# Self-attention scores of a fused decoder layer, made for two key heads at a time instead of one

## The chip, the cores and the metric

The kernel runs on one core of a Trainium2 chip. The metric is the device time of one launch in microseconds (us); three launches of the kernel before were timed. The engines of the core run side by side and meet at semaphores: TensorE (PE, with its weight loads listed as PEld), VectorE (DVE), ScalarE (ACT), GpSimd (POOL) and SyncE (SP), which issues the DMAs.

## What is computed

A decoder layer for 8 sequences of 128 positions with 512 features, in float32: layer norm and causal self-attention, cross-attention over a context, and a feed-forward part. The change concerns only the scores of the self-attention, which has 32 query heads of 16 features and 8 key heads, four query heads to each key head. Cut to what matters:

```python
q = q * cos + _rotate_half(q) * sin
k = k * cos + _rotate_half(k) * sin
qg = q.reshape(b, HKV, G, t, DH)              # HKV = 8, G = 4, DH = 16
scores = einsum('bhgtd,bhkd->bhgtk', qg, k) / sqrt(DH)
scores = where(causal, scores, finfo(float32).min)
attn = softmax(scores, axis=-1)
ctx = einsum('bhgtk,bhkd->bhgtd', attn, v)
```

## The kernel before

**Arithmetic.** Every float32 product is made of three matmuls of a reduced-precision type: each operand is held as a high part (suffix h) and the remainder (suffix l), and `split3` (L217) issues high x high (L219), high x low (L220) and low x high (L221). ScalarE writes each high part (`hi`, L982), VectorE each low part (`lo`, L1218).

**Stages.** A self-attention stage runs over the 8 sequences (`batch`, one call to a sequence; seven go through a hardware loop, the last is written out). Behind it come a cross-attention stage and a feed-forward stage, which the change doesn't touch. A batch also makes the keys and values that its sequence needs in the cross-attention (`cross_values`, `cross_keys`), and the projections of the next sequence (`turn_xn`, `q_product`, `kv_product`, `turn_qk`).

**Scores.** `scores(b, j)` makes the scores of key head j with its four query heads: 128 queries by 4 x 128 keys, one PSUM bank, bank 2 + j % 3. First a matmul of the identity with the mask writes the causal mask into the bank (L645, 128 rows of the array); then three matmuls of `split3` add the products. The keys stand in `Kbdh` and `Kbdl`, block by block on a diagonal, two key heads to a tile of 128 rows: tile m = j // 2, rows 0 to 63 for even j and 64 to 127 for odd j. So each of these products uses 64 rows of the array. VectorE then takes the maxima (`maxima`, L1338, L1341), ScalarE the exponentials and their sums (`probs`, L1039, into `Pa`), VectorE the reciprocals (L1346), GpSimd multiplies (`normalise`, L472). TensorE turns the result (`turn`, L672), ScalarE and VectorE split it into `PTah` and `PTal`, and `values` multiplies by the values `Vbdh`, `Vbdl`.

**Order.** It is written out by hand and every engine runs its own list in order. Of sequence b + 1, `scores` 0, 1 and 2 are made in the closing part of batch b: 0 and 1 behind `cross_values(0)`, then four transpositions of the second layer norm's result `xn2` (L750), then scores 2, then `cross_keys(0)`, `cross_keys(1)`, `cross_values(1)`. In the steps j = 0 to 7 of a batch, `turn(j)` is followed by `scores(b, j + 3)` for j up to 4, then by `values(j - 1)`; `turn_context` and `turn_xn` stand in step 1, `q_product` in steps 3 and 4, `kv_product` in 5 and 6. `cross_keys(0)` waits for both halves of `HTl` (L1218), which VectorE makes when ScalarE has written `HTh` from the transpositions of L750. In front of scores j >= 3 TensorE waits for the exponentials of j - 3, whose bank it takes.

Of the kernel before, what the change touches and what calls it, by code (L numbers as in the profile page):

```python
# [33 lines left out]
P = 128  # L34
# [26 lines left out]
def decoder_layer(nc, x, ctx, s_wq, s_wk, s_wv, s_wo, x_wq, x_wk, x_wv, x_wo, gate_w, up_w, down_w,  # L61
                  fc1_w, fc2_w, expert_w, gamma, beta, rope, out):
    with ExitStack() as stack:
# [153 lines left out]
        def split3(pe, dst, lh, ll, rh, rl, start, stop):  # L217

            pe.matmul(dst, lh, rh, start=start, stop=False)  # L219
            pe.matmul(dst, lh, rl, start=False, stop=False)  # L220
            return pe.matmul(dst, ll, rh, start=False, stop=stop)  # L221
# [340 lines left out]
        def _(pe):  # L562
# [67 lines left out]
                                    HTh[:, kc, :], HTl[:, kc, :], kc == 0, kc == KC - 1)  # L630
                op.then_inc(pe_kvp, 1)

            def scores(b, j):

                bk = bank[2 + j % 3]
                m, r = j // 2, 64 * (j % 2)
                if j >= 3:

                    pe.wait_ge(a_exp, SKV * b + j - 2)
                elif j < 2:  # L640

                    pe.wait_ge(v_qkl, 2 * b + 2)
                pe.wait_ge(g_kbd, KC * b + m + 1)
                pe.wait_ge(v_kbd, KC * b + m + 1)
                pe.matmul(bk[:].rearrange("p (c k) -> p c k", c=SG), ident_r[:],  # L645
                          mask_r[:].unsqueeze(1).to_broadcast([P, SG, P]), start=True, stop=False)
                rows = slice(r, r + 64)
                split3(pe, bk[:], QTh[rows, m, :], QTl[rows, m, :], Kbdh[rows, m, :], Kbdl[rows, m, :],
                       False, True).then_inc(pe_s, 1)

            def queries(g_count, head, pair, bk):

# [9 lines left out]
            def batch(b, last):  # L662
                def turn(j):

                    pe.wait_ge(g_norm, SKV * b + j + 1)
                    if j >= 2:
                        pe.wait_ge(v_ptl, SKV * b + j - 1)
                    elif j == 0:

                        pe.wait_ge(v_kvl, 4 * b + 3)  # L670
                    for c in range(SG):
                        op = pe.transpose(bank[5 + j % 2][:, c * P:(c + 1) * P],  # L672
                                          Pa[:, j % 3, c * P:(c + 1) * P], ident[:])
                    op.then_inc(pe_pt, 1)

                def values(j):

                    if j == SKV - 1:
                        for n, split in enumerate((v_ptl_half, v_ptl)):
                            pe.wait_ge(split, SKV * b + SKV if n else b + 1)  # L680
                            cols = slice(n * KEYS, (n + 1) * KEYS)
                            op = split3(pe, bank[7][:, cols], Vbdh[:, j * P:(j + 1) * P], Vbdl[:, j * P:(j + 1) * P],
                                        PTah[:, j % 2, cols], PTal[:, j % 2, cols], False, n == 1)
                        op.then_inc(pe_pv, 1)
                        return
                    pe.wait_ge(v_ptl, SKV * b + j + 1)
                    if j == 0:
                        pe.wait_ge(v_vl, b + 1)
                        pe.wait_ge(a_v, b + 1)
                    op = split3(pe, bank[7][:], Vbdh[:, j * P:(j + 1) * P], Vbdl[:, j * P:(j + 1) * P],  # L690
                                PTah[:, j % 2, :], PTal[:, j % 2, :], j == 0, False)

                for j in range(SKV):
                    turn(j)
                    if j + 3 < SKV:
                        scores(b, j + 3)
                    if j == 5 and not last:
                        kv_product((0, 1))  # L700
                    if j == 6 and not last:
                        kv_product((2, 3))
                    if j == 7:

                        pe.wait_ge(v_htl, 2 * b + 1)

                        pe.wait_ge(g_xw, 2)
                        cross_values(0, (0,))
                    if j == 1:

                        pe.wait_ge(v_kvl, 4 * b + 4)
                        turn_context(b)
                    if j >= 1:
                        values(j - 1)
                    if j == 1 and not last:
                        turn_xn(b + 1)
                    if j == 3 and not last:

                        pe.wait_ge(v_xnl, b + 2)
                        pe.wait_ge(v_htl, 2 * b + 1)  # L720
                        q_product((0, 1))
                    if j == 4 and not last:
                        q_product((2, 3))
                values(SKV - 1)
                if not last:

                    pe.wait_ge(a_exp, SKV * b + SKV)
                    turn_qk(b + 1, q_rot)

                for g in range(SG):  # L730
                    if g % 2 == 0:
                        pe.wait_ge(v_ol if g else v_ol_half, b + 1)
                    op = split3(pe, bank[6][:], OTh[:, g * P:(g + 1) * P], OTl[:, g * P:(g + 1) * P], SOh[:, g, :],
                                SOl[:, g, :], g == 0, g == SG - 1)
                op.then_inc(pe_wo, 1)
                cross_values(0, (1, 2, 3))
                if last:

                    pe.wait_ge(st_xt, 32 * NB)
                    queries(1, 0, 0, QBANK[0])  # L740
                    queries(2, 1, 0, QBANK[0])
                else:
                    scores(b + 1, 0)
                    scores(b + 1, 1)

                    pe.wait_ge(v_vl, b + 2)

                pe.wait_ge(v_xn2, b + 1)
                for kc in range(KC):
                    op = pe.transpose(bank[0][:, kc * P:(kc + 1) * P], xn2[:, kc * P:(kc + 1) * P], ident[:])  # L750
                op.then_inc(pe_ht, 1)

                pe.wait_ge(v_kvl, 4 * b + 5)
                if last:
                    queries(3, 2, 0, QBANK[1])
                    queries(4, 3, 0, QBANK[1])
                else:
                    scores(b + 1, 2)
                cross_keys(0, b)
                cross_keys(1, b)  # L760

                cross_values(1, range(KC))
# [20 lines left out]

            pe.wait_ge(v_c, 4)
            scores(0, 0)
            scores(0, 1)

            pe.wait_ge(v_w, 7)
            scores(0, 2)
            pe.wait_ge(v_w, 10)  # L790
            with pe.Fori(0, NB - 1) as b:
                batch(b, False)
# [422 lines left out]
        def _(dve):  # L1215
# [132 lines left out]
            def batch(b, last, stats_ahead):  # L1348
# [41 lines left out]
                if not last:  # L1390
                    maxima(b + 1, 0)
                    maxima(b + 1, 1)
                    maxima(b + 1, 2)
                    diagonal_keys(b + 1, (2, 3))
                    reciprocals_a(b + 1, 0)
                    reciprocals_a(b + 1, 1)
                cross_keys_lo(b, 0)
                if stats_ahead:
                    ln1_stats(b + 2)
                cross_keys_lo(b, 1)  # L1400
# [230 lines left out]
```

## Time and profile before

| | |
|---|---|
| median of 3 timed launches | 1129.45 us (1128.24 to 1130.34) |
| profiled execution, first to last instruction (span) | 1126.2 us |
| profiled execution, its own device time | not listed apart; the timed median is 3.3 us over the span |
| TensorE busy | 1077.5 us (96%) |
| VectorE busy | 665.5 us (59%) |
| ScalarE busy | 545.4 us (48%) |
| GpSimd busy | 388.5 us (34%) |
| mean granted TensorE clock | 0.981 of full |

A matmul's busy time is from its start to its modelled end, and matmuls overlap in the pipeline; so the distance from one start to the next tells what one costs, and the busy share of TensorE is near 100% wherever it doesn't wait. The self-attention stage lies between about 26 and 380 us of the span.

### The profile page before, as it was taken

The page shows a single profiled execution, that of the slowest core. Times are in us where ns is not written, and L with a number is a line of the kernel's source. Part 1 is how long each engine was busy: PE and PEld are TensorE (multiplying, and loading weights), DVE is VectorE, ACT ScalarE, POOL GpSimd, SP SyncE. Part 2 cuts the span into 40 slices and gives each one's busy share as a digit, 9 for nine tenths or more (in the row PEclk, how much of TensorE's full clock was granted, in tenths as well). Part 3 has the DMA queues.
Part 4 walks back from the last instruction along what each step waited for, and adds up shares of the span by engine and source line. Part 5 has one row for each costly group of instructions (what it writes and reads, how often), then busy time and mean ns, then how long its engine had stood idle before and what let it go on. Part 6 is the DMA issues. An engine that isn't in the chain of part 4 may idle for free.

```text
span 1126.2 us, 20373 instructions
## 1 busy us (share of the span) xinstructions
PE 1077.5 (96%) x7000; PEld 950.0 (84%) x7000; DVE 665.5 (59%) x1441; ACT 545.4 (48%) x1651; POOL 388.5 (34%) x393
## 2 busy tenths in 40 slices
PE   4899999999999999999999999999999999999997
PEld 4577777777776899999899998999999999899996
DVE  6776776776765465555555554655555555646554
ACT  4536545545546364554554554645546446632121
POOL 4523332332333352342432432523425226621110
PEclk8599999999999999999999999999999999999999
DMA  7002202202206311221110311111302022300000
GB/s 252 10 19 84 102 19 84 102 19 84 103 19 206 132 58 40 65 69 55 58 38 29 104 57 39 57 48 56 103 20 75 20 70 90 95 20 19 19 19 19
DMA packets 48976, 72.52 MB, mean 64 GB/s; under 512 B 3344, under 2 KB 28688, under 8 KB 48912
## 3 DMA queue, kind: packets, MB, share of 16 engines
q1 hardware_dynamic: 48912, 71.61, 19.4%
q8 instruction: 47, 0.77, 0.3%
q14 instruction: 17, 0.14, 0.0%
HBM read 48.53 MB, written 18.87 MB: 60 GB/s over the span
## 4 chain that ended last, share of the span: by engine, by line
PE 82%; DVE 8%; issue 4%; ACT 3%; POOL 2%; DVEq 0%; POOLq 0%; ACTq 0%
PE bank L219 25%; PE bank L221 23%; PE bank L220 23%; PE bank L874 4%; PE bank L672 2%; POOL Kbdh L457 2%; PE bank L645 1%; DVE PTal L1218 1%; DVE b_nb L1447 1%; DVE xn L1386 1%; ACT Pb L1113 1%; DVE b_max L1444 1%; DVE Kbdl L1309 1%; ACT PTah L982 1%; DVE kr L1291 0%
## 5 line engine op out<-in xcount | busy, mean ns | idle before, releaser
L509 POOL TENSOR_TENSOR Pb<-Pb,b_rec 128x512 f32<-128x512 f32 x128 | 133.2, 1041 | 373.1 <-DVE b_rec L1451 372.7
L219 PE MATMUL bank<-XTh,WQh 128*128 128x256 f32 x512 | 146.0, 285 | 4.3 <-DVE Ql L1218 4.3
L220 PE MATMUL bank<-XTl,WQh 128*128 128x256 f32 x512 | 144.7, 283 | 0.0
L221 PE MATMUL bank<-XTh,WQl 128*128 128x256 f32 x512 | 144.6, 282 | 0.0
L1113 ACT ACTIVATE Pb<-bank,b_nb 128x256 f32<-128x256 f32 x256 | 119.0, 470 | 30.9 <-DVE b_nb L1447 29.8
L982 ACT ACTIVATE PTh<-bank 128x512 fp32r<-128x512 f32 x128 | 76.6, 598 | 101.1 <-PE bank L874 100.7
L1218 DVE TENSOR_TENSOR Ol<-bank,Oh 128x256 fp32r<-128x256 f32 x128 | 53.7, 419 | 117.5 <-ACT Oh L982 117.4
L472 POOL TENSOR_TENSOR Pa<-Pa,a_rec 128x512 f32<-128x512 f32 x64 | 66.3, 1040 | 148.7 <-DVE a_rec L1346 148.7
L1039 ACT ACTIVATE Pa<-bank,a_nb 128x128 f32<-128x128 f32 x256 | 90.9, 380 | 50.4 <-DVE a_nb L1341 50.0
L219 PE MATMUL bank<-WOh,Oh 128*128 128x512 f32 x256 | 110.8, 433 | 1.1 <-DVE x_res L1461 1.1
L219 PEld LDWEIGHTS bank<-XTh,WQh 128*128 128x128 f32 x512 | 97.1, 190 | 9.6 <-DVE Ql L1218 5.2
L220 PEld LDWEIGHTS bank<-XTl,WQh 128*128 128x128 f32 x512 | 97.5, 190 | 4.8
L221 PE MATMUL bank<-WOh,Ol 128*128 128x512 f32 x256 | 100.8, 394 | 0.0
L220 PE MATMUL bank<-WOl,Oh 128*128 128x512 f32 x256 | 100.1, 391 | 0.0
L221 PEld LDWEIGHTS bank<-XTh,WQl 128*128 128x128 f32 x512 | 97.3, 190 | 0.0
L982 ACT ACTIVATE Oh<-bank 128x256 fp32r<-128x256 f32 x128 | 49.0, 383 | 96.5 <-PE bank L221 90.3
L1218 DVE TENSOR_TENSOR PTl<-bank,PTh 128x512 fp32r<-128x512 f32 x128 | 88.1, 688 | 9.9 <-ACT PTh L982 1.4
L1444 DVE TENSOR_REDUCE b_max<-bank 128x2 f32<-128x512 f32 x128 | 87.1, 681 | 6.6 <-PE bank L221 6.5
L1218 DVE TENSOR_TENSOR Ql<-bank,Qh 128x512 fp32r<-128x512 f32 x64 | 44.0, 691 | 78.6 <-ACT Qh L982 78.6
L219 PE MATMUL bank<-KV,Qh 128*128 128x256 f32 x256 | 72.9, 285 | 4.8 <-issue 2.9
L874 PE MATMUL bank<-ident,Pb 128*128 128x128 f32 x512 | 76.9, 273 | 0.3 <-POOL Pb L509 0.3
L219 PE MATMUL bank<-PTh,KV 128*128 128x256 f32 x256 | 72.5, 283 | 0.3 <-DVE Ol L1218 0.3
(235 smaller groups left out, 3050.8 us busy)
## 6 DMA issues: line engine op xcount, KB each, us to landing
kv_scratch<-KVst SPq DMA_DIRECT2D x8, 2048.0 KB, 7.2
KV<-kv_scratch SPq DMA_DIRECT2D x32, 512.0 KB, 3.4
raw<-in_L_xattn_Wo_dram SPq DMA_DIRECT2D x32, 256.0 KB, 3.3
raw<-in_L_xattn_Wq_dram SPq DMA_DIRECT2D x24, 256.0 KB, 4.1
cx<-in_ctx_dram SPq DMA_DIRECT2D x8, 256.0 KB, 5.2
XTh<-HTh SPq DMA_DIRECT2D x8, 256.0 KB, 2.7
XTl<-HTl SPq DMA_DIRECT2D x8, 256.0 KB, 2.8
raw_first<-in_L_xattn_Wq_dram SPq DMA_DIRECT2D x8, 256.0 KB, 7.3
```

The source lines that it names most:

```text
L219: pe.matmul(dst, lh, rh, start=start, stop=False)
L220: pe.matmul(dst, lh, rl, start=False, stop=False)
L221: return pe.matmul(dst, ll, rh, start=False, stop=stop)
L457: gp.tensor_tensor(Kbdh[:, m, :].rearrange("p (c k) -> p c k", c=SG), src, bd_mask[:].unsqueeze(2).to_broadcast([P, SG, P]), ALU.mult).the ...
L472: gp.tensor_tensor(pj, pj, a_rec[:, SG * j:SG * j + SG].unsqueeze(2).to_broadcast([P, SG, P]), ALU.mult).then_inc(g_norm, 1)
L509: gp.tensor_tensor(pk, pk, b_rec[:, k % 4, :].unsqueeze(2).to_broadcast([P, 2, KEYS]), ALU.mult).then_inc(b_g_norm, 1)
L874: op = pe.transpose(bank[3 + k % 2][:, c * KEYS + h * P:c * KEYS + (h + 1) * P], Pb[:, k % 4, h, c * P:(c + 1) * P], ident[:])
L982: return act.activation(dst, src, ACT.Copy)
L1039: op = act.activation(Pa[:, j % 3, c * P:(c + 1) * P], bank[2 + j % 3][:, c * P:(c + 1) * P], ACT.Exp, bias=a_nb[:, h:h + 1], scale=S_SCAL ...
L1113: op = act.activation(Pb[:, k % 4, h, :], bank[k % 3][:, h * KEYS:(h + 1) * KEYS], ACT.Exp, bias=b_nb[:, k % 4, h:h + 1], scale=X_SCALE, a ...
L1218: return dve.tensor_tensor(dst, src, f32(hi_part), ALU.subtract)
L1444: dve.tensor_reduce(b_max[:, k % 4, :], bank[k % 3][:].rearrange("p (h k) -> p h k", h=2), AX.X, ALU.max).then_inc(b_v_mx, 1)
```

## The change

`scores(b, m)` now takes the two key heads of tile m at once: the masks into both banks, then the three 64-row products of the first, then the three of the second. The waits for the keys stand behind the masks. Four calls serve a sequence. Pair 0 stands where scores 0 and 1 stood; pair 1 (key heads 2 and 3) stands between `cross_keys(0)` and `cross_keys(1)` of the batch before; pair 2 follows `turn(1)`, pair 3 follows `turn(3)`. A pair waits for the exponentials of head 2m - 2, the last whose bank it takes. On VectorE the maxima of head 2 move behind the low part of `cross_keys(0)`. Ahead of the first batch, pair 1 now waits for the exponentials of head 0. The number of matmuls is the same.

```diff
@@ -630,23 +630,24 @@
                                     HTh[:, kc, :], HTl[:, kc, :], kc == 0, kc == KC - 1)
                 op.then_inc(pe_kvp, 1)
 
-            def scores(b, j):
-
-                bk = bank[2 + j % 3]
-                m, r = j // 2, 64 * (j % 2)
-                if j >= 3:
-
-                    pe.wait_ge(a_exp, SKV * b + j - 2)
-                elif j < 2:
+            def scores(b, m):
+
+
+                halves = [(bank[2 + (2 * m + n) % 3], slice(64 * n, 64 * n + 64)) for n in range(2)]
+                if m:
+
+                    pe.wait_ge(a_exp, SKV * b + 2 * m - 1)
+                else:
 
                     pe.wait_ge(v_qkl, 2 * b + 2)
+                for bk, _ in halves:
+                    pe.matmul(bk[:].rearrange("p (c k) -> p c k", c=SG), ident_r[:],
+                              mask_r[:].unsqueeze(1).to_broadcast([P, SG, P]), start=True, stop=False)
                 pe.wait_ge(g_kbd, KC * b + m + 1)
                 pe.wait_ge(v_kbd, KC * b + m + 1)
-                pe.matmul(bk[:].rearrange("p (c k) -> p c k", c=SG), ident_r[:],
-                          mask_r[:].unsqueeze(1).to_broadcast([P, SG, P]), start=True, stop=False)
-                rows = slice(r, r + 64)
-                split3(pe, bk[:], QTh[rows, m, :], QTl[rows, m, :], Kbdh[rows, m, :], Kbdl[rows, m, :],
-                       False, True).then_inc(pe_s, 1)
+                for bk, rows in halves:
+                    split3(pe, bk[:], QTh[rows, m, :], QTl[rows, m, :], Kbdh[rows, m, :], Kbdl[rows, m, :],
+                           False, True).then_inc(pe_s, 1)
 
             def queries(g_count, head, pair, bk):
 
@@ -694,8 +695,8 @@
 
                 for j in range(SKV):
                     turn(j)
-                    if j + 3 < SKV:
-                        scores(b, j + 3)
+                    if j in (1, 3):
+                        scores(b, (j + 3) // 2)
                     if j == 5 and not last:
                         kv_product((0, 1))
                     if j == 6 and not last:
@@ -741,7 +742,6 @@
                     queries(2, 1, 0, QBANK[0])
                 else:
                     scores(b + 1, 0)
-                    scores(b + 1, 1)
 
                     pe.wait_ge(v_vl, b + 2)
 
@@ -754,9 +754,9 @@
                 if last:
                     queries(3, 2, 0, QBANK[1])
                     queries(4, 3, 0, QBANK[1])
-                else:
-                    scores(b + 1, 2)
                 cross_keys(0, b)
+                if not last:
+                    scores(b + 1, 1)
                 cross_keys(1, b)
 
                 cross_values(1, range(KC))
@@ -783,10 +783,9 @@
 
             pe.wait_ge(v_c, 4)
             scores(0, 0)
+
+            pe.wait_ge(v_w, 7)
             scores(0, 1)
-
-            pe.wait_ge(v_w, 7)
-            scores(0, 2)
             pe.wait_ge(v_w, 10)
             with pe.Fori(0, NB - 1) as b:
                 batch(b, False)
@@ -1390,11 +1389,12 @@
                 if not last:
                     maxima(b + 1, 0)
                     maxima(b + 1, 1)
-                    maxima(b + 1, 2)
                     diagonal_keys(b + 1, (2, 3))
                     reciprocals_a(b + 1, 0)
                     reciprocals_a(b + 1, 1)
                 cross_keys_lo(b, 0)
+                if not last:
+                    maxima(b + 1, 2)
                 if stats_ahead:
                     ln1_stats(b + 2)
                 cross_keys_lo(b, 1)
```

In the closing part of a batch TensorE had these rows before (names carry buffer numbers; `xn2` is the second layer norm's result, bank6 takes `cross_keys(0)`):

```order
L750 MATMUL bank0<-ident_50,xn2_93 128x128 x4
L753 REGISTER_ALU
L643 REGISTER_ALU
L645 MATMUL bank4<-mask_r_95,ident_r_51 128x512
L219 MATMUL bank4<-Kbdh_80,QTh_81 128x512
L220 MATMUL bank4<-Kbdl_84,QTh_81 128x512
L221 MATMUL bank4<-Kbdh_80,QTl_85 128x512
L219 MATMUL bank6<-HTh_83,XKh_71 128x256
L220 MATMUL bank6<-HTl_87,XKh_71 128x256
```

and has these now:

```order
L750 MATMUL bank0<-ident_50,xn2_93 128x128 x4
L753 REGISTER_ALU
L219 MATMUL bank6<-HTh_83,XKh_71 128x256
L220 MATMUL bank6<-HTl_87,XKh_71 128x256
L221 MATMUL bank6<-HTh_83,XKl_72 128x256
```

Nothing is left between the transpositions and the first product of `cross_keys(0)`. Further on, between `cross_keys(0)` and `cross_keys(1)`, the new rows are these (the first row is the last product of `cross_keys(0)`):

```order
L221 MATMUL bank6<-HTh_83,XKl_72 128x256
L639 ISA
L644 MATMUL bank4<-mask_r_95,ident_r_51 128x512
L644 MATMUL bank2<-mask_r_95,ident_r_51 128x512
L646 REGISTER_ALU
L219 MATMUL bank4<-Kbdh_80,QTh_81 128x512
L220 MATMUL bank4<-Kbdl_84,QTh_81 128x512
L221 MATMUL bank4<-Kbdh_80,QTl_85 128x512
L219 MATMUL bank2<-Kbdh_80,QTh_81 128x512
L220 MATMUL bank2<-Kbdl_84,QTh_81 128x512
L221 MATMUL bank2<-Kbdh_80,QTl_85 128x512
L219 MATMUL bank7<-HTh_83,XKh_71 128x256
```

So key head 3 (bank2) is done here and no longer in step 0 of the next batch. In steps 0 and 1 of a batch TensorE had, from `turn(0)` on (bank5), these rows:

```order
L672 MATMUL bank5<-ident_50,Pa_88 128x128 x4
L643 REGISTER_ALU
L645 MATMUL bank2<-mask_r_95,ident_r_51 128x512
L219 MATMUL bank2<-Kbdh_80,QTh_81 128x512
L220 MATMUL bank2<-Kbdl_84,QTh_81 128x512
L221 MATMUL bank2<-Kbdh_80,QTl_85 128x512
L665 REGISTER_ALU
L672 MATMUL bank6<-ident_50,Pa_88 128x128 x4
L645 MATMUL bank3<-mask_r_95,ident_r_51 128x512
L219 MATMUL bank3<-Kbdh_80,QTh_81 128x512
L220 MATMUL bank3<-Kbdl_84,QTh_81 128x512
L221 MATMUL bank3<-Kbdh_80,QTl_85 128x512
```

and has now, from the same place:

```order
L673 MATMUL bank5<-ident_50,Pa_88 128x128 x4
L666 REGISTER_ALU
L673 MATMUL bank6<-ident_50,Pa_88 128x128 x4
L639 REGISTER_ALU
L644 MATMUL bank3<-mask_r_95,ident_r_51 128x512
L644 MATMUL bank4<-mask_r_95,ident_r_51 128x512
L219 MATMUL bank3<-Kbdh_80,QTh_81 128x512
L220 MATMUL bank3<-Kbdl_84,QTh_81 128x512
L221 MATMUL bank3<-Kbdh_80,QTl_85 128x512
L219 MATMUL bank4<-Kbdh_80,QTh_81 128x512
L220 MATMUL bank4<-Kbdl_84,QTh_81 128x512
L221 MATMUL bank4<-Kbdh_80,QTl_85 128x512
```

Both turns stand together, and pair 2 with its two banks behind them; the context's transposition (bank1) follows.

## Rows read from the trace of the kernel before

**Rows 1.** The page: busy us, share of the span, instructions of each engine.

```profile
PE 1077.5 (96%) x7000; PEld 950.0 (84%) x7000; DVE 665.5 (59%) x1441; ACT 545.4 (48%) x1651; POOL 388.5 (34%) x393
```

**Rows 2.** Windows; columns as its first line has them.

```profile
core 0: us, PE busy (x) PEld busy (x) DVE busy (x) ACT busy (x) POOL busy (x), PEclk, DMA share, GB/s
26.00:60.00 34.00, 26.76 (x74) 16.80 (x75) 23.97 (x41) 18.69 (x70) 16.62 (x12) 0.56 0.03 9
60.00:350.00 290.00, 282.15 (x1522) 216.80 (x1521) 206.64 (x463) 149.15 (x573) 97.18 (x96) 1.00 0.20 70
118.15:122.40 4.25, 3.90 (x15) 2.09 (x15) 2.59 (x6) 0.94 (x2) 2.73 (x3) 1.00 0.00 0
387.00:390.10 3.10, 1.16 (x8) 0.77 (x6) 2.00 (x8) 2.05 (x9) 0.85 (x1) 1.00 0.40 148
390.10:393.50 3.40, 3.16 (x16) 3.16 (x17) 2.03 (x5) 2.22 (x7) 1.62 (x3) 0.57 0.73 229
393.50:397.00 3.50, 3.50 (x30) 3.50 (x30) 2.27 (x3) 1.27 (x3) 3.10 (x3) 0.93 0.13 45
```

**Rows 3.** TensorE timeline, step 3: start, us, instruction.

```profile
138.61 0.60 PE L672 MATMUL bank<-ident,Pa 128*128 128x128 f32 x4
138.97 0.48 PE L645 MATMUL bank<-mask_r,ident_r 128*128 128x512 f32 x1
139.38 0.50 PE L219 MATMUL bank<-Kbdh,QTh 64*128 64x512 f32 x1
139.72 0.38 PE L220 MATMUL bank<-Kbdl,QTh 64*128 64x512 f32 x1
139.94 0.39 PE L221 MATMUL bank<-Kbdh,QTl 64*128 64x512 f32 x1
140.26 0.50 PE L219 MATMUL bank<-PTah,Vbdh 128*128 128x512 f32 x1
140.60 0.40 PE L220 MATMUL bank<-PTal,Vbdh 128*128 128x512 f32 x1
```

**Rows 4.** TensorE timeline, closing part of a batch, and first turn of the next.

```profile
117.70 0.39 PE L645 MATMUL bank<-mask_r,ident_r 128*128 128x512 f32 x1
118.02 0.49 PE L219 MATMUL bank<-Kbdh,QTh 64*128 64x512 f32 x1
...
120.58 0.63 PE L750 MATMUL bank<-ident,xn 128*128 128x128 f32 x4 [0.28 <-DVE xn L1386]
...
121.27 0.47 PE L645 MATMUL bank<-mask_r,ident_r 128*128 128x512 f32 x1
...
122.56 0.39 PE L219 MATMUL bank<-HTh,XKh 128*128 128x256 f32 x1
...
131.17 0.60 PE L672 MATMUL bank<-ident,Pa 128*128 128x128 f32 x4
```

**Rows 5.** VectorE timeline over the same stretch.

```profile
121.95 0.76 DVE L1218 TENSOR_TENSOR HTl<-bank,HTh 128x256 fp32r<-128x256 f32 x2 [0.92 <-ACT HTh L982]
...
132.00 0.69 DVE L1218 TENSOR_TENSOR KVst<-bank,KVst 128x512 fp32r<-128x512 f32 x1 [1.98 <-ACT KVst L982]
132.93 0.69 DVE L1338 TENSOR_REDUCE a_max<-bank 128x4 f32<-128x512 f32 x1 [0.24 <-PE bank L221]
...
135.89 0.69 DVE L1218 TENSOR_TENSOR PTal<-bank,PTah 128x512 fp32r<-128x512 f32 x1 [0.18 <-ACT PTah L982]
```

**Rows 6.** ScalarE timeline, high part of turn(1).

```profile
135.25 0.61 ACT L982 ACTIVATE PTah<-bank 128x512 fp32r<-128x512 f32 x1
```

**Rows 7.** GpSimd timeline, head 3 normalised.

```profile
136.74 1.04 POOL L472 TENSOR_TENSOR Pa<-Pa,a_rec 128x512 f32<-128x512 f32 x1 [5.60 <-DVE a_rec L1346]
```

**Rows 8.** TensorE timeline in the first batch, at half clock.

```profile
47.40 0.77 PE L219 MATMUL bank<-PTah,Vbdh 128*128 128x512 f32 x1 [2.91 <-DVE PTal L1218]
...
50.38 0.78 PE L645 MATMUL bank<-mask_r,ident_r 128*128 128x512 f32 x1
...
52.66 0.79 PE L219 MATMUL bank<-PTah,Vbdh 128*128 128x512 f32 x1
```

## The prediction

> **What bounds the kernel now.** I read the page's busy shares first: TensorE has 96% of the span, VectorE, the next, 59% [rows 1]. Then windows: between 60 and 350 us, where seven batches' worth of self-attention runs, TensorE is busy 282.15 of 290 us at full clock, so it waits for 7.85 us in all [rows 2]. Here the reader is to see that TensorE's own rhythm sets the time, and that any work taken off it counts, unless a wait takes its place. The rhythm is regular: the first turn of a batch starts at 131.17 [rows 4], one period is 41.8 us (an estimate: 290 us by seven is 41.4, the timeline repeats at 41.8). Last, the timeline of TensorE start by start. The reader is to look at distances between starts, not at durations.
>
> **What a visit to the 64-row products costs.** In step 3 the starts are 138.97 (mask), 139.38, 139.72, 139.94 (the three products), 140.26 and 140.60 (the next two full products) [rows 3]. The one distance between like neighbours is 0.22 to 0.23. The others are 0.41, 0.34, 0.32 and 0.34: beyond 0.23 each they add 0.18, 0.11, 0.09 and 0.11. Of the 0.18, half comes from following a transposition: behind a full product the mask's distance is 0.32 (117.70 to 118.02) [rows 4]. So going from 128 rows to 64 costs 0.20, coming back 0.20, together **0.40 us for each visit**. The trace doesn't say why; the start that follows a switch is late and so is the one behind it. The Trainium skill, TensorEngine Tiling (Array Packing), Key Properties, says that a change of tiling mode drains the engine and that a change of tile alone does not; the rows agree with the first half by their 0.40.
>
> **What the change takes off TensorE.** Eight visits a batch become four: 4 x 0.40 = 1.60 us. Where the last product of the first half hands over to the first of the second half, the rows have no example. Bounds: nothing is gained if the hand-over takes the 0.23 of neighbours [rows 3]; 0.23 is gained if they stream together. They use rows 0 to 63 and 64 to 127 and write different banks, and nothing in the program orders them, so I take 0.23: 4 x 0.23 = 0.92. A hand-over as dear as a switch would cost 0.20 instead. Masks issued side by side cost 0.23 each as before. In all 2.52 us of each batch's TensorE time, if nothing gave it back. With the end of the first half unchanged, a pair lasts 1.99 us behind a transposition, against 1.29 for one head (138.97 to 140.26).
>
> **What gives it back, in order of the batch.**
>
> *Ahead of `xn2`.* Pair 0 is followed by the transpositions of `xn2`, which already wait for VectorE (120.58, 0.28 idle) [rows 4]. That chain starts with the output projection and takes nothing from the scores. Pair 0 ends 0.40 + 0.23 = **0.63** sooner and the wait grows from 0.28 to 0.91.
>
> *Ahead of `cross_keys(0)`.* Its first product needs the first half of `HTl`. VectorE starts the two halves at 121.95, 0.76 for both [rows 5], behind ScalarE's `HTh`, behind the `xn2` transpositions. The first half is done near 122.35, TensorE could go on at 122.42. Before, scores 2 filled 121.27 to 122.56 [rows 4], and the wait was hidden. Now nothing stands there: **1.15** us idle. Pair 1 doesn't fill it, since it comes behind the 24 products. Queued behind this wait is all of TensorE's list: `cross_keys`, `cross_values(1)`, the next batch.
>
> *Steps 1 and 2.* Head 3 is done ahead, which brings `turn(0)`, `turn(1)`, pair 2, the context's transposition, `values(0)`, `turn_xn`, `turn(2)` and `values(1)` close together. Before, `turn(0)` to `turn(3)` took 138.61 - 131.17 = 7.44 us, of it three visits at 1.29; the other work is 3.57 us [rows 3, 4]. With pair 2 it makes 5.56. But `turn(3)` needs head 3 normalised. VectorE comes to its maximum only behind the low part of `cross_values(1)`, which starts 0.83 behind `turn(0)` (132.00) and holds it 0.61: 1.44. From the maximum (132.93) over ScalarE's exponentials and `PTah` (135.25), VectorE's `PTal` (135.89) and reciprocal, to the end of GpSimd's multiply (136.74 + 1.04 = 137.78) it is 4.85 us [rows 5 to 7]. So `turn(3)` starts 1.44 + 4.85 + 0.06 = 6.35 behind `turn(0)`, and TensorE waits **0.8** us, partly at `values(1)` for `PTal`, partly at `turn(3)`. From `turn(4)` on nothing is late: the q products lie ahead of it.
>
> Sum of a period: -2.52 + 0.63 + 1.15 + 0.8 = +0.06; following the starts one by one I get +0.2, and take **+0.2** for six periods: +1.2 us. Last batch: `turn(0)` comes 1.9 later than before (pair 1 lies ahead of it), and the shortened steps give back 1.1, since from `turn(4)` on the chain over VectorE, ScalarE and GpSimd sets the pace there: +0.8. First batch: up to `values(0)` it waits for VectorE until 47.40 with 2.91 idle [rows 8], which stays; behind it three visits, at half clock 2.28 (50.38 to 52.66), about 1.9 (across the rise of the clock) and 1.3, 5.5 in all, give way to one pair of about 3.3 at half clock: -2.2. Elsewhere nothing moves: cross-attention and feed-forward have the same lists. These terms make +1.2 + 0.8 - 2.2 = **-0.2 us**: the change would do nothing.
>
> **The clock.** The cross-attention stage has one lull: between 387.0 and 390.1 TensorE is busy 1.16 of 3.10 us. Right behind it the clock is granted at half (1.2 GHz) from 390.1 to 393.5, and 16 matmuls are done in 3.4 us where the next 3.5 us have 30 [rows 2]: such a fall costs 1.6 us. In the closing part of a batch, 118.15 to 122.40, TensorE was busy 3.90 of 4.25 us, at full clock [rows 2]. After the change this stretch holds the six 64-row products (the first 1.5 us), 0.91 idle, four transpositions, 1.15 idle. Its last 3 us are as empty as that lull. I expect the clock to fall in some of the seven closings and not in all, as the lull may be placed differently against whatever decides it; nearly half, **three**, at 1.6 us: **+4.8 us**. Bounds: none (0) and all seven (+11.2). The half-clock stretch then lies on `cross_keys(0)` and pair 1, where TensorE is the bound, so nothing hides it. The Trainium skill, TensorE: Matmul & The Clock Gate, Why this matters for your kernels, asks that matmul bursts have no long idle gaps between them; two gaps of about 1 us would by themselves pass by its advice, and by it the sum would stay at -0.2.
>
> **Sum.** -0.2 + 4.8 = +4.6 us on the profiled span of 1126.2, which lies 3.3 under the median of 1129.45: 1134.0.
>
> **The rivals.**
>
> *The clock holds, halves overlap* (chance 0.18). For it: before, these closings had only 64-row products and transpositions around a 0.28 wait and kept full clock. Against it: the lull at 387 is no emptier. Time 1129.3, no difference.
>
> *Halves don't stream together, clock falls* (0.21). The hand-over takes 0.23. Pairs 1 and 3 then lose it in full, pair 2 partly (it only shortens the 0.8 wait), pair 0 not at all: +0.45 a period, +3.2 in all: 1137.2. With a hand-over of +0.20 more, about 1140 (0.04 of its own). With the clock held, 1132.5 (0.06).
>
> *Faster: both halves' three products run side by side* (0.08). Then a pair saves 0.69 and not 0.23; pairs 1 and 3 give 0.92 more a period, -6.5 in all: 1127.5 with three falls, 1122.8 with none. It decides from about -0.9 a period on if the clock falls, at -0.35 if it holds. Against it: a head's products follow each other in the list and the three of one half stand together, so only neighbours across the hand-over can meet. The Trainium skill, TensorE: Matmul & The Clock Gate, Part 3, says of products in different row groups that they run together but start and end in program order; by that the gain is one product a pair, as taken.
>
> **How the numbers follow.** Forecast (overlap by one product, clock falls two to four times) 0.43. The range must hold the no-change case and the one without overlap: 1128.8 to 1138.5. A difference of 0.2% is 2.3 us, about what a measurement of this kernel tells from none. Slower than 1131.7: most of the forecast (0.38), 0.21, 0.04, 0.05: 0.68, less a little for a term I haven't seen: 0.65. Same: 0.24. Faster: 0.11.
>
> **What would show it.** In the changed profile: TensorE waits of about 0.9 at L750 for VectorE's `xn`, about 1.1 ahead of the first `cross_keys` product for `HTl`, seven times each; waits of 0.3 to 0.5 for `PTal` and `Pa` in each batch; second halves whose first product starts within 0.05 us of the last of the first half; and slices of half clock between 100 and 360 us, each right behind a closing part. I am wrong if the clock row stays full there, if cross keys start without a wait, or if distances inside a pair show more than one overlap.

## The result: 1134.66 us, slower by 0.57%

| | before | changed |
|---|---|---|
| median of 5 timed launches | 1129.0 us (1128.24 to 1130.34) | 1134.66 us (1133.94 to 1134.83) |
| ratio, 95% interval | | 1.0057 (1.0041 to 1.0072) |
| span of the profiled execution | 1126.2 us | 1132.5 us (+6.3) |
| mean granted TensorE clock | 0.981 | 0.976 |

The forecast was 1134.0. The number is met; the way to it is not, as the rows show, so the close agreement is luck. Of the +6.3 us of the span, the self-attention stage, the only one that the change touches, gives +1.2. The rest arises in the cross-attention stage behind it, whose list is the same.

The page of the changed kernel, busy times and the clock row, beside [rows 1]:

```profile
PE 1055.6 (93%) x7000; PEld 941.3 (83%) x7000; DVE 668.1 (59%) x1441; ACT 544.7 (48%) x1651; POOL 388.7 (34%) x393
PEclk9699999989999999999999999999999999999999
```

TensorE is busy 21.9 us less with as many instructions, and still the kernel is slower: what it saved it now waits, and more.

TensorE's waits between 30 and 372 us of the changed kernel (in total, times, longest):

```profile
PE bank L219 <- DVE PTal L1217: 13.8, 25, 4.9
PE bank L750 <- DVE xn L1385: 9.5, 7, 1.4
PE bank L219 <- DVE HTl L1217: 9.2, 7, 1.3
PE bank L644 <- ACT Pa L1038: 3.1, 1, 3.1
PE bank L673 <- POOL Pa L472: 2.4, 10, 0.2
```

The two waits of the closing part are there, seven times each, 1.35 us ahead of `xn2` and 1.32 ahead of `cross_keys(0)`. Read the start times too. This is TensorE's timeline at pair 1, from its two masks to the product behind it (a row with x2 merges two matmuls of one line; its time is the start of the first):

```profile
82.36 0.63 PE L644 MATMUL bank<-mask_r,ident_r 128*128 128x512 f32 x2
82.92 0.51 PE L219 MATMUL bank<-Kbdh,QTh 64*128 64x512 f32 x2
83.26 0.41 PE L220 MATMUL bank<-Kbdl,QTh 64*128 64x512 f32 x2
83.50 0.40 PE L221 MATMUL bank<-Kbdh,QTl 64*128 64x512 f32 x2
83.83 0.39 PE L219 MATMUL bank<-HTh,XKh 128*128 128x256 f32 x1
```

This was the surprise. The list has A1 A2 A3 B1 B2 B3 (A is the half on rows 0 to 63, B the one on 64 to 127), but the view shows A1 and B1 as one group: two products in 0.51 us where one alone takes 0.50 [rows 3]. Product by product the starts of the two halves lie within 0.02 us. **All three run side by side**, and six products take 0.91 us (82.92 to 83.83), as three did. A pair lasts 1.47 us behind a full product where I had said 1.99 behind a transposition.

The closing part and the steps behind it, one batch each:

```profile
118.64 0.63 PE L750 MATMUL bank<-ident,xn 128*128 128x128 f32 x4 [1.35 <-DVE xn L1385]
120.59 0.36 PE L219 MATMUL bank<-HTh,XKh 128*128 128x256 f32 x1 [1.32 <-DVE HTl L1217]
```

```profile
89.57 1.03 PE L673 MATMUL bank<-ident,Pa 128*128 128x128 f32 x8
92.75 0.47 PE L219 MATMUL bank<-PTah,Vbdh 128*128 128x512 f32 x1 [0.19 <-DVE PTal L1217]
95.90 0.66 PE L673 MATMUL bank<-ident,Pa 128*128 128x128 f32 x4 [0.24 <-POOL Pa L472]
```

`turn(3)` starts 6.33 us behind `turn(0)`; I had worked out 6.35. Windows of 6 us from the start of `cross_keys(0)` in the seven closings (columns as in [rows 2]), and of one pair of lulls with all that lies between:

```profile
78.11:84.11 6.00, 6.00 (x34) 5.22 (x35) 4.08 (x11) 3.50 (x17) 2.08 (x2) 0.75 0.31 87
120.59:126.59 6.00, 6.00 (x45) 5.22 (x46) 4.66 (x12) 3.42 (x18) 2.08 (x2) 1.00 0.31 87
161.80:167.80 6.00, 6.00 (x45) 5.22 (x46) 4.66 (x12) 3.42 (x18) 2.08 (x2) 1.00 0.30 87
203.00:209.00 6.00, 6.00 (x33) 5.24 (x34) 3.89 (x11) 3.50 (x17) 2.08 (x2) 0.72 0.30 87
245.60:251.60 6.00, 6.00 (x26) 5.58 (x26) 3.19 (x9) 3.41 (x17) 2.08 (x2) 0.50 0.31 87
289.50:295.50 6.00, 5.98 (x33) 5.22 (x34) 3.97 (x11) 3.50 (x17) 2.08 (x2) 0.73 0.30 87
332.10:338.10 6.00, 5.96 (x45) 5.21 (x46) 4.67 (x12) 3.39 (x17) 2.08 (x2) 1.00 0.30 87
199.66:202.96 3.30, 0.63 (x4) 0.45 (x5) 2.38 (x4) 0.60 (x1) 2.10 (x2) 1.00 0.00 0
547.20:551.00 3.80, 3.78 (x23) 3.78 (x24) 1.72 (x4) 2.33 (x7) 0.54 (x1) 0.70 0.02 4
```

The clock fell in four of seven closings, one of them for twice the length: five lengths of 3.4 us at half (1.2 GHz). It is the clock column that tells, beside the instructions done in the same 6 us: 45, 33 or 34, 26. All seven closings have a stretch like that of the last row but one in front of them, 0.63 us busy of 3.30, and three kept full clock behind it.

The last row is in the untouched stage. TensorE's timeline at the two turns of the cross-attention loop, of the changed kernel:

```profile
543.71 0.39 PE L221 MATMUL bank<-WOh,Ol 128*128 128x512 f32 x1
547.22 0.38 PE L219 MATMUL bank<-KV,Qh 128*128 128x256 f32 x1 [3.13 <-issue]
...
700.09 0.39 PE L221 MATMUL bank<-WOh,Ol 128*128 128x512 f32 x1
703.61 0.38 PE L219 MATMUL bank<-KV,Qh 128*128 128x256 f32 x1 [3.13 <-issue]
```

and of the kernel before:

```profile
542.42 0.39 PE L221 MATMUL bank<-WOh,Ol 128*128 128x512 f32 x1
544.13 0.38 PE L219 MATMUL bank<-KV,Qh 128*128 128x256 f32 x1 [1.33 <-issue]
...
695.53 0.39 PE L221 MATMUL bank<-WOh,Ol 128*128 128x512 f32 x1
697.51 0.38 PE L219 MATMUL bank<-KV,Qh 128*128 128x256 f32 x1 [1.59 <-issue]
```

"issue" says that nothing in the profile was waited for. Each turn stalls 3.13 us in place of 1.33 and 1.59: 1.80 + 1.54 = 3.3 us. Right behind the first stall the clock falls once more (0.70 in the window 547.20 to 551.00). The changed kernel is behind by 1.29 us ahead of the first turn (543.71 to 542.42), by 3.09 at it, 4.56 ahead of the second (700.09 to 695.53) and 6.10 at it: 1.47 of this comes between the turns, and that is the fall.

### The profile page after: what moved, and what is told of

It is laid out like the page before. It is cut to its first block, busy times and chain, and to the rows that moved or that the text cites. A ratio compares the mean times of both kernels' runs of the same rounds, so it can differ in the third digit from the quotient of the medians.

```text
span 1132.5 us, 20349 instructions
## 1 busy us (share of the span) xinstructions
PE 1055.6 (93%) x7000; PEld 941.3 (83%) x7000; DVE 668.1 (59%) x1441; ACT 544.7 (48%) x1651; POOL 388.7 (34%) x393
## 4 chain that ended last, share of the span: by engine, by line
PE 70%; issue 13%; DVE 7%; POOL 6%; ACT 4%; POOLq 0%; DVEq 0%; ACTq 0%
PE bank L219 21%; PE bank L221 21%; PE bank L220 21%; PE bank L873 4%; POOL Kbdh L457 3%; POOL Pa L472 2%; PE bank L673 1%; DVE PTal L1217 1%; DVE b_nb L1447 1%; ACT Pb L1112 1%; DVE b_max L1444 1%; DVE Kbdl L1308 1%; ACT Pa L1038 1%; ACT PTah L981 1%; DVE kr L1290 0%
```

## The experiments

Names: "half" is a fall of the clock to half for 3.4 us. All are the changed kernel with the edit given, except `b_head`, an edit of the kernel before. Times are medians of several launches; rows and stalls come from one profiled launch of each. Where "+6" stands, six idle semaphore increments follow the self-attention stage on TensorE (see the first). The kernel before was timed beside each group: 1128.69 us for `a_shift6`, `a_inter`, `a_moves` and `a_fill`, 1128.84 for `a_fillx`, `a_fillk`, `a_shift3` and `b_head`, 1129.59 for `a_mask2` and `a_maskx2`. The changed kernel itself was not timed again.

### 1. The place of the loop head (a_shift6)

Theory 1: the stall at a turn depends on where the loop's head lies in TensorE's stream of instructions. Counted from the start of TensorE's program, two instructions to a matmul, the head (its first instruction) lies at 1241 before and at 1235 after the change. The Trainium skill, Runtime: NRT & Kernel Launch, Instruction fetch mechanics, says that instructions are fetched in blocks of 256 and that a taken branch to a block that isn't held makes the engine wait. Rival: the pairs leave something behind that slows the later stage.

```diff
             batch(NB - 1, True)
+            for _ in range(6):
+                pe.sem_inc(pad_sem, 1)
```

> The changed kernel, with six semaphore increments on TensorE between the self-attention stage and the cross-attention loop. They do nothing but bring the first instruction of that loop back to the place in TensorE's instruction stream that it has in the kernel before. Theory 1 (the two stalls of 3.13 us at the turns of that loop, and the clock fall behind the first, come from where the loop's first instruction stands): both stalls go back to 1.3 to 1.6 us, no half clock near 550 us, and the time drops by 5 us, to about 1129.7. Theory 2 (the stalls are the chance of one execution, or come from the data transfers, which were shifted by 1.2 us): they stay near 3.1 us in some or all executions, and the time stays at 1134.7 within 1 us.

Measured: 1128.61 us (1125.41 to 1130.72, 11 runs), ratio 1.000 (0.9989 to 1.0011). At the first turn:

```profile
542.11 0.39 PE L221 MATMUL bank<-WOh,Ol 128*128 128x512 f32 x1
543.70 0.38 PE L219 MATMUL bank<-KV,Qh 128*128 128x256 f32 x1 [1.20 <-issue]
```

The second turn stalls 1.41, and no fall follows the first. Six instructions that do nothing take 6.0 us off, and theory 1 holds. Not all of the 6.0 is theirs: of the 6.9 us between the two profiled spans (1132.5 and 1125.6) 5.2 lie at the two turns and in the fall between them, and 1.6 were there before the first turn, where the falls of the clock happened to lie elsewhere. Without its effect on a loop it never touched, the change makes no difference.

### 2. How sharp the place is (a_shift3)

The same with three increments, the head at 1238.

> The changed kernel with three idle semaphore increments on TensorE ahead of the cross-attention loop, so that the loop's head lies half way between its place of before and of after (1238). If the stall grows step by step with the place, the two turns stall between 1.3 and 3.1 us each, about 2.2; if there is an edge, either 1.2 to 1.7 (about 1128 to 1129) or 3.1 (about 1134). Rival: the three instructions themselves cost nothing either way, and a stall of 3.1 would show that it is not the number of instructions but the exact place.

Measured: 1130.28 us (1126.18 to 1135.18, 10 runs), ratio 1.0014 (0.9994 to 1.0033); the turns stall 1.24 and 1.57 us. The stall changes between 1235 and 1238, and at 1238 it is already what it was at 1241: an edge, and no slope beyond it. The kernel with six increments spreads over 5.3 us too, and the one before, timed with it, over 5.4. The number of halves of a launch explains only a part: in `a_shift6` launches of 1127.88 and 1130.72 us have the same mean clock, 0.976, and the slowest of `a_shift3`, 1135.18, has 0.975 where others with 0.976 take 1130.3. The rest of the spread is open.

### 3. The other way round: the kernel before with its head displaced (b_head)

```diff
+            for _ in range(250):
+                pe.sem_inc(pad_sem, 1)
             pe.wait_ge(g_const, 6)
```

> The kernel before with 250 idle semaphore increments at the very start of TensorE's program, where it waits 7.87 us for its first tile. 250 is 256 less 6: if instructions are fetched in blocks of 256, as the Trainium skill's page Runtime: NRT & Kernel Launch states in Instruction fetch mechanics, the head of the cross-attention loop lies in its block where the changed kernel has it, and the two turns stall 3.1 us each, with or without a fall of the clock behind: 1132 to 1135 (3.4 to 6 us over the kernel before). If the place in a block is not what counts, the stalls stay 1.3 to 1.6 us and the time at 1129, provided that the increments are hidden in the first wait; if they are not hidden, the first product of the page starts later than 7.87 us by what they cost.

Measured: 1164.95 us, ratio 1.0314 (1.028 to 1.0348). Its increments (first and last start), and rows of its timeline:

```profile
L766 PEldq EVENT_SEMAPHORE  x250: 51/51/51, 0.8 to 39.1; - x125
39.41 3.65 PE L574 MATMUL bank<-ident,rawQ 128*128 128x128 f32 x16 [39.41 <-issue]
...
579.40 0.38 PE L219 MATMUL bank<-KV,Qh 128*128 128x256 f32 x1 [3.24 <-issue]
```

The increments were hidden only in part: they run from 0.8 to 39.1 us, and the first product starts at 39.41 and not 7.87, so 31.5 of the 36.1 us over before are theirs, and 4.6 are left. The turns stall 3.24 and 3.27 us (1.91 and 1.68 more than before), with a half behind the first, in a kernel that has none of the change. 250 more is 256 less 6. So the long stall comes back where the place within blocks of 256 is that of the changed kernel, which agrees with the Trainium skill's blocks; no other displacement of this kernel was run, and fetching itself is in no trace.

### 4. The order of the six products (a_inter, +6)

Theory 1: the halves run side by side in whatever order they stand. Rival: the alternating order A1 B1 A2 B2 A3 B3 is needed for a full overlap, or costs a hand-over at each step.

```diff
-                for bk, rows in halves:
-                    split3(...)
+                for n, (lh, rh) in enumerate(((QTh, Kbdh), (QTh, Kbdl), (QTl, Kbdh))):
+                    for bk, rows in halves:
+                        op = pe.matmul(bk[:], lh[rows, m, :], rh[rows, m, :], start=False, stop=n == 2)
```

> The changed kernel with the same six increments, and the six products of a pair in alternating order: first of one half, first of the other, second, second, third, third. Theory 1 (products of different halves of the array run side by side whatever their order in a pair): a pair still lasts 1.47 us, and the time is that of the changed kernel with the increments, about 1129.7, within 1 us. Theory 2 (the order three and three costs something that the alternating order does not, such as a late first product or late semaphores): a pair gets shorter by 0.1 to 0.2 us, or the first half's maxima come 0.2 us later; the time moves by 1 to 3 us.

Measured: 1127.03 us (1124.29 to 1130.53, 10 runs), ratio 0.9992 (0.9975 to 1.0008). Pair 1:

```profile
79.99 0.63 PE L645 MATMUL bank<-mask_r,ident_r 128*128 128x512 f32 x2
80.55 0.51 PE L651 MATMUL bank<-Kbdh,QTh 64*128 64x512 f32 x2
80.89 0.40 PE L651 MATMUL bank<-Kbdl,QTh 64*128 64x512 f32 x2
81.13 0.40 PE L651 MATMUL bank<-Kbdh,QTl 64*128 64x512 f32 x2
81.46 0.39 PE L219 MATMUL bank<-HTh,XKh 128*128 128x256 f32 x1
```

1.47 us again, to the hundredth, and a period of 41.17 (`xn2` at 116.27, 157.43, 198.60), as in the changed kernel. The order among the six costs and gives nothing. The first turn stalls 2.12 us here, with the head where `a_shift6` has it and stalls 1.20: a good place has stalls of different length too.

### 5. The moves without the pairing (a_moves, +6)

Pairs stand where the change puts them, but each mask stands directly ahead of its own three products.

```diff
-                for bk, _ in halves:
-                    pe.matmul(bk ... mask_r ..., start=True, stop=False)
                 pe.wait_ge(g_kbd, KC * b + m + 1)
                 pe.wait_ge(v_kbd, KC * b + m + 1)
                 for bk, rows in halves:
+                    pe.matmul(bk ... mask_r ..., start=True, stop=False)
                     split3(...)
```

> The changed kernel with the same six increments, where everything stays where the change put it, but each half of a pair has its mask directly ahead of its own three products, as before. Theory 1 (what the change gains is fewer switches between 128 and 64 rows and halves side by side): two halves take 2.6 us and not 1.47. Pairs 1 and 3 lose 1.1 us each in full, pair 2 about 0.7, pair 0 nothing (hidden in the wait for xn2): 2.9 us a period, some 20 us in all, less what falls of the clock are saved where the wait for xn2 shrinks to 0.2 us: about 1147, with 1143 to 1151 covered. Theory 2 (the profile only models the ends and starts of such products, and the pairing gains little): at most 1137.

Measured: 1143.13 us, ratio 1.0134 (1.0114 to 1.0155). Pair 1, first rows of each half and what follows:

```profile
81.05 0.39 PE L647 MATMUL bank<-mask_r,ident_r 128*128 128x512 f32 x1
...
82.26 0.49 PE L647 MATMUL bank<-mask_r,ident_r 128*128 128x512 f32 x1
82.68 0.50 PE L219 MATMUL bank<-Kbdh,QTh 64*128 64x512 f32 x1
...
83.58 0.39 PE L219 MATMUL bank<-HTh,XKh 128*128 128x256 f32 x1
```

2.53 us for the two heads against 1.47: 1.06 less by the pairing. If the visit saved is worth the 0.40 of the prediction, 0.66 is left for three products under three others (3 x 0.23 = 0.69). A full mask between the halves keeps them apart. The moves alone make a period of 43.3, 1.5 over before; the pairing takes 2.1 back (I had expected 2.9, and 1147 us in place of 1143.13). The wait for `xn` is 0.28 here, as before, and the one for `HTl` 1.32: the wait ahead of `cross_keys(0)` comes from the move, the one ahead of `xn2` from the pairing.

I had also expected fewer falls here, as the wait for `xn` is short. There are none fewer: five lengths in four closings, as in the changed kernel. The 3.30 us ahead of `cross_keys(0)` and the 6 us behind its start, in one of them:

```profile
162.72:166.02 3.30, 1.70 (x8) 0.93 (x8) 2.38 (x4) 0.60 (x1) 2.11 (x2) 0.90 0.00 0
166.02:172.02 6.00, 6.00 (x26) 5.56 (x27) 3.21 (x9) 3.40 (x17) 2.08 (x2) 0.50 0.30 87
```

So the clock falls behind a wait of 0.29 us and one of 1.32, with TensorE busy for half of the stretch. It doesn't take two long waits.

### 6. The lulls and the clock (a_fill, a_fillx, a_fillk)

Theory 1: the falls come from the closing part, where 0.63 us of work stand in 3.30 (changed kernel). Rival: they have another cause, and filling a lull costs time or changes nothing. The filler is four mask products into bank 5, whose result is thrown away; `a_fill` has it ahead of both waits.

```diff
+            def fill():
+                for _ in range(4):
+                    pe.matmul(bank[5] ... mask_r ..., start=True, stop=True)
...
+                if not last:
+                    fill()
                 pe.wait_ge(v_xn2, b + 1)
...
+                if not last:
+                    fill()
                 cross_keys(0, b)
```

> The changed kernel with eight extra matmuls a batch (mask by identity into bank 5, which nobody reads then): four ahead of the wait for xn2, four between the xn2 transpositions and the first product of the cross-attention keys. They add 0.9 us of work into each of two waits of 1.35 and 1.32 us, so they delay nothing; the loop of the cross-attention stage starts 8 instructions later than in the kernel before. Theory 1 (the clock falls because TensorE does too little between pair 0 and the cross keys): the clock stays full between 60 and 370 us, each period takes 41.2 us, and the time is 5 to 7 us under that of the changed kernel with the increments, about 1123, if the loop's place is a good one. Theory 2 (the falls have another cause, such as the 64-row products themselves): four or five falls stay, and the time is as without the extra matmuls, within 1 us, or higher.

Measured: 1121.33 us (1120.13 to 1122.28), ratio 0.9937 (0.9921 to 0.9953), and no half between 60 and 380 us. 56 products more, and 7.3 us less than `a_shift6`. The head, at 1249 here, is at a good place: 1.24 and 1.68 at the turns.

Then each lull alone: `a_fillx` fills only the one ahead of `xn2`,

> The changed kernel with four extra mask products (results unused, in the bank that turn(0) overwrites) ahead of the wait for xn2 only; the wait ahead of cross_keys(0) stays open, about 1.3 us. The head of the cross-attention loop lies at 1242 in TensorE's instructions, one off the place of the kernel before, so its turns should stall 1.2 to 1.7 us. Theory 1, the clock falls because two lulls stand close together: one filled is enough, no half clock between 60 and 380 us, 1121 to 1123. Theory 2, the lull ahead of cross_keys(0) is the one that counts (the half clock starts behind it): falls stay in some closings, 1126 to 1130. Theory 3, a lull of 1.3 us counts wherever it stands: fewer falls than four, between the two.

and `a_fillk` only the one ahead of `cross_keys(0)`.

> The same with the four extra products ahead of cross_keys(0) only; the wait for xn2 stays open, about 1.35 us. Theory 1: no falls, 1121 to 1123, as when the other lull alone is filled. Theory 2: no falls either, while filling the other alone leaves them. Rival, the lull ahead of xn2 is the one that counts: falls in some closings, 1126 to 1130.

Measured: 1121.05 (1120.38 to 1122.82), ratio 0.9933 (0.9913 to 0.9954), and 1120.5 (1120.15 to 1121.81), ratio 0.9929 (0.9902 to 0.9955). One lull filled is enough, whichever it is. The lull that stays, in `a_fillx` and in `a_fillk`:

```profile
118.40 0.36 PE L219 MATMUL bank<-HTh,XKh 128*128 128x256 f32 x1 [1.32 <-DVE HTl L1224]
```

```profile
116.37 0.63 PE L755 MATMUL bank<-ident,xn 128*128 128x128 f32 x4 [1.38 <-DVE xn L1392]
```

In these two kernels one open wait of 1.3 to 1.4 us left the clock alone. `a_moves` has one such wait too, and its clock fell: there the other wait, ahead of `xn2`, is short because the unpaired 64-row products take longer, and not because full-array products fill it. So filling either lull with four full products stops the falls, which is shown; that two open waits are needed is not so; and what sets `a_moves` apart from `a_fillx` (1.70 us busy of the 3.30 ahead of `cross_keys(0)` against 1.82) no run shows.

### 7. Real work in the lull (a_mask2, a_maskx2)

The first mask of pair 1 writes bank 4, which is free when `cross_keys(0)` waits for `HTl`. It is moved there. `a_mask2` has +6, `a_maskx2` the filler ahead of `xn2` instead.

```diff
+                if not last:
+                    mask(bank[4])
                 cross_keys(0, b)
                 if not last:
-                    scores(b + 1, 1)
+                    scores(b + 1, 1, 1)
```

> The changed kernel with the first mask of pair 1 (bank 4, free by then) moved from behind cross_keys(0) into the lull ahead of it, and six idle semaphore increments ahead of the cross-attention loop (head at 1240). The wait for HTl should fall from 1.32 to about 1.0 and the mask's 0.23 to 0.30 us leave the busy part: 1.6 to 2 us less over seven batches than the changed kernel with the increments (1125.6 span). Theory A, the clock needs more in the lull than one matmul: falls as before, 3 to 5 lengths of 3.4 us, about 1127. Theory B, one matmul in the lull is enough to hold the clock: no falls, 1119 to 1121.

> The same early mask, but with the four extra products ahead of the wait for xn2 instead of the increments (head at 1241). With that lull filled no closing had a fall, at 1121.05. The early mask should take 0.23 us off each of seven batches: 1119.5 (1118.5 to 1120.5). If the time stays at 1121, the mask was not on the path: the wait for HTl would then shrink by 0.3 without the period getting shorter.

Measured: `a_mask2` **1119.24 us** (1118.93 to 1119.94), ratio 0.9912 (0.9883 to 0.994); `a_maskx2` 1119.99 (1118.92 to 1120.66), ratio 0.992 (0.9891 to 0.9948). The closing part of `a_mask2`, and a window over the two lulls of another batch that answers to 199.66 to 202.96 of the changed kernel:

```profile
116.84 0.63 PE L754 MATMUL bank<-ident,xn 128*128 128x128 f32 x4 [1.37 <-DVE xn L1393]
117.35 0.50 PE L635 MATMUL bank<-mask_r,ident_r 128*128 128x512 f32 x1
118.69 0.39 PE L219 MATMUL bank<-HTh,XKh 128*128 128x256 f32 x1 [0.84 <-DVE HTl L1225]
```

```profile
197.22:200.44 3.22, 1.00 (x5) 0.60 (x5) 2.30 (x4) 0.60 (x1) 2.12 (x2) 1.00 0.00 0
```

Theory B (one matmul in the lull holds the clock) holds nearly: with one useful product in the lull one closing of seven has a half (the first) and six have none. The period is 40.84 to 40.91 us without a fall, 0.3 under the changed kernel's. This version does no extra matmul and beats both kernels: 0.9% under before, 1.4% under the change (1119.24 to 1134.66, timed on different occasions). A part of it is the clock in the untouched stage: the profile of `a_mask2` has no fall at the lull of [rows 2] (387.00 to 393.50), which the kernel before, the changed one and `a_maskx2` have. With the other lull filled as well nothing more is gained: the two times overlap. The window holds 1.00 us of work where the changed kernel had 0.63.

## Why the prediction was right, and where it was not

In the span I said +4.6 and got +6.3. The device time of an execution lies 2.3 us over its span (1134.78 to 1132.5), not 3.3: my figure was the median of before less one span, and 1 us of it was that execution's being a short one. With 2.3 the same sum gives 1133.1.

**The visit, 0.40 us: right.** From the first mask of pair 1 (82.36) to the second full product behind it (84.06) 1.70 us pass; two masks, three products (0.23 each) and one product of 256 columns (0.12) make 1.27 of it, which leaves 0.43.

**The hand-over: mis-sized, and the largest error of the sum.** I allowed one product of overlap, 0.23, and took three as a rival of 0.08, since "only neighbours across the hand-over can meet". They meet across the list: 0.66 a pair measured (2.53 - 1.47 - 0.40), near the 0.69 of three neighbours. Against my 0.23 that is 0.46 more for each of pairs 1 and 3, 0.9 a period, as the rival had it. The period without a fall is 41.2 us (the transpositions of `xn2` start at 118.64, 159.85 and 201.01; 41.17 in `a_inter`), against 41.80 before: -0.6, where I said +0.2.

**Ahead of `xn2`: mechanism right, size off.** 1.35 and not 0.91, since pair 0 ends 1.06 sooner (0.28 + 1.06 = 1.34) and not 0.63. **Ahead of `cross_keys(0)`: right.** 1.32 for my 1.15, and the same whether the pairs overlap or not (`a_inter`, `a_moves`).

**Steps 1 and 2: right.** `turn(3)` falls 6.33 us behind `turn(0)` for my 6.35, set by the chain over VectorE, ScalarE and GpSimd, whatever the pair takes. The waits that the profile lists there, 0.19 and 0.24, are less than my 0.8, but by the starts TensorE loses more, an estimate: pair 2 takes 1.55 (90.36 to 91.91), the other work 3.57 as I had it, and 6.33 - 5.12 = 1.2 us is the wait, 0.8 and the 0.44 by which the pair came out shorter. The list counts idle time only from a matmul's modelled end.

**First and last batch:** -2.6 for -2.2 and, up to the last `xn2`, +0.6 for +0.8. The first of these is in part luck with the clock, which the sum didn't have. It came back to full sooner, as one window of the kernel before and of the changed one shows:

```profile
53.80:56.20 2.40, 2.40 (x9) 1.66 (x8) 1.14 (x3) 1.99 (x9) 1.04 (x1) 0.52 0.00 0
53.80:56.20 2.40, 2.40 (x15) 1.49 (x14) 1.02 (x3) 1.31 (x7) 0.86 (x1) 1.00 0.00 0
```

These 2.4 us at full clock are worth about 1.2 us, an estimate from the doubled speed; some 1.4 of the 2.6 are then left for the rearrangement.

**The clock: right in kind and nearly in size.** Three halves at 1.6 were said; five lengths came, in four closings. The periods with one are 42.47, 42.63 and 42.61, that with two 43.94, so 1.30, 1.46, 1.44 and 2.77 over 41.17: 7.0 us for my 4.8. Experiment 6 shows that the emptiness of the closing part is the cause, by the falls that go when a lull is filled. The picture of two lulls of about 1 us was too narrow: `a_moves` has one, 1.32 us, and the clock fell there as often. What the Trainium skill, TensorE: Matmul & The Clock Gate, Why this matters for your kernels, asks is that no long gap stand between bursts; by it the clock would have stayed, and the runs had it fall behind waits of 1.35 and 1.32 us.

The stage sums so: -2.6 (first batch) - 3.8 (six periods at -0.63) + 7.0 (clock) + 0.6 (last batch) = +1.2, the measured difference at the last `xn2`. My own terms made +4.6 there.

**What I had not seen at all: +5 us in the cross-attention loop.** The step that failed is "Elsewhere nothing moves: cross-attention and feed-forward have the same lists". The lists are the same, their addresses are not. The errors are 3.4 us too much in the stage and 5.1 missed behind it, which leaves 1.7; the 1.0 in the device time hid more of it. Without the stalls the time is that of `a_shift6`, 1128.61, no difference, near the 1127.5 of the rival with all products side by side and three falls. That rival, to which I gave 0.08, had the mechanism. The forecast was met because an overlap set too small and a stall not seen at all nearly cancel.

## What to carry to other kernels

When TensorE is the bound, work that is pulled off it ahead of a wait only makes the wait longer, and such lulls, even short ones, can cost more clock than the work was worth: read the granted clock behind them, and move some useful matmul, even one, into the gap. Products on disjoint rows that write different banks ran under each other in both orders tried, and not when a full-array matmul stood between them. After any change of the instruction count, look at the "issue" stalls of every loop behind it before blaming or praising the edit.

## What the runs showed of the hardware

- Three 64-row products of one half of the array and three of the other take 0.91 us together and 0.88 alone (139.38 to 140.26, [rows 3]); the second half starts with the first although it stands three products later in the list. The Trainium skill, TensorE: Matmul & The Clock Gate, Part 3, has matmuls start and end in the order of the program; these starts don't agree with it.
- At the turn of its longest loop TensorE stalls 1.2 to 2.1 us (most often 1.2 to 1.7; 1.90 in `a_maskx2` and 2.12 in `a_inter`) or 3.1 to 3.3 us. A displacement of the loop's head by 3 instructions out of some 1240 decides between the two, and one of 250 in the kernel before brings the long stall too.
- The long stall was followed by a fall of the clock at the first turn (0.70 over 3.8 us in the changed kernel; in `b_head` too), and not at the second.
- In which closings the clock falls differs between kernels with the same closing part (`a_shift6`: six lengths, `a_inter`: two); what decides it is open. The clock fell also with TensorE busy for 1.70 of the 3.30 us ahead (`a_moves`), where the products were of 64 rows.
- An idle semaphore increment took TensorE 0.154 us when nothing else was waited for (250 of them start from 0.8 to 39.1 us in `b_head`).
